# A four-layer graph network on one core: batch norm ahead and folded into weights, a fused ELU, and log-softmax by chunk and tile

## What is computed

```python
# second block, after two convolutions
return jax.nn.log_softmax(h, axis=1)
# third block
h = (x @ W).reshape(N, H, C)                      # 4 heads of 32
...                                               # attention weights alpha from x @ W and att_src, att_dst
out = jax.ops.segment_sum(h[src] * alpha[:, :, None], dst, num_segments=N).reshape(N, H * C)
out = out + x @ W_res + bias
out = (out - bn_mean) * jax.lax.rsqrt(bn_var + BN_EPS) * bn_gamma + bn_beta
return jax.nn.elu(out)
```

## Time and profile before

| | us |
|---|---|
| median of 3 runs | 2975.74 |
| the runs | 2973.39 to 2977.03 |
| the profiled execution | 2972.53 |
| its span | 2970.7 |
| TensorE busy in it | 2514.9 (85%) |
| VectorE busy | 2453.1 (83%) |
| ScalarE busy | 1969.7 (66%) |

### The profile page before, as it was taken

One profiled execution on the slowest core, in us unless ns is written; L12 is line 12 of the kernel. 1 busy time (PEld: TensorE's weight loads), 2 busy tenths in 40 slices (PEclk: granted clock), 3 DMA queues, 4 the chain that ended last, 5 costly groups with the idle time before them and its releaser, 6 DMA issues. The chain is left out here.

```text
span 2970.7 us, 60024 instructions
## 1 busy us (share of the span) xinstructions
PE 2514.9 (85%) x19214; PEld 2069.2 (70%) x19214; DVE 2453.1 (83%) x5349; ACT 1969.7 (66%) x3974; POOL 222.5 (7%) x487
## 2 busy tenths in 40 slices
PE   0888888775489888789884799999999999989998
PEld 0555555554467666667663599979998799979997
DVE  7998999953579999899997788868887788878886
ACT  1666666640368888788884577766777677767775
POOL 3000000000000000000000111101110111101110
PEclk9998999987788999899997899999999999999999
DMA  1232332355123333633330343414333243324332
GB/s 44 77 119 108 114 126 101 134 240 131 74 101 109 109 109 109 182 118 111 109 109 5 124 148 129 150 69 150 136 133 129 96 148 129 130 91 144 137 134 83
DMA packets 86664, 349.26 MB, mean 118 GB/s; under 512 B 47241, under 2 KB 59329, under 8 KB 59584
## 3 DMA queue, kind: packets, MB, share of 16 engines
q1 hardware_dynamic: 86437, 346.34, 33.2%
HBM read 279.61 MB, written 65.67 MB: 116 GB/s over the span
## 5 line engine op out<-in xcount | busy, mean ns | idle before, releaser
L1902 ACT ACTIVATE awcol<-aturned 125x500 fp32r<-125x500 f32 (+2 forms) x652 | 373.9, 573 | 310.7 <-PE aturned L1809 307.4
L1999 DVE TENSOR_TENSOR awcol<-aturned,awcol 125x500 fp32r<-125x500 f32 (+2 forms) x652 | 427.7, 656 | 114.7 <-ACT awcol L1902 109.3
L1821 PE MATMUL asum<-awcol,vals_high 125*128 125x512 f32 (+1 forms) x1300 | 477.6, 388 | 0.0
L1389 PE MATMUL gturned<-ident,grow 125*125 125x125 f32 x2500 | 409.7, 305 | 3.8 <-ACT grow L1299 3.8
L1821 PE MATMUL asum<-awcol,vals_low 125*128 125x256 f32 x1300 | 402.8, 319 | 0.0
L1389 PEld LDWEIGHTS gturned<-ident,grow 125*125 125x125 f32 x2500 | 332.5, 204 | 81.7 <-issue 77.1
L1226 DVE CUSTOM_DVE_ANT_0 grow<-grow,bias 125x3125 f32<-125x3125 f32 x100 | 341.7, 3417 | 25.1 <-DMA bias<-bias_dram 10.9
L1217 DVE SCALAR_TENSOR_TENSOR grow<-line,a_dst 125x3125 f32<-125x3125 f32 x100 | 347.6, 3476 | 13.2 <-PE gturned L1389 13.2
L1299 ACT ACTIVATE grow<-grow,neg 125x3125 f32<-125x3125 f32 x100 | 290.5, 2905 | 90.6 <-DVE neg L1229 90.5
L1339 PE MATMUL gparts<-gwcol,h_mem 125*32 125x125 f32 x5000 | 244.0, 290 | 106.1 <-ACT gwcol L1312 106.1
L1312 ACT ACTIVATE gwcol<-gturned 125x1000 f32<-125x1000 f32 x300 | 281.8, 1002 | 17.6 <-PE gturned L1389 17.5
(11 more groups left out here) (312 smaller groups left out, 5016.9 us busy)
## 6 DMA issues: line engine op xcount, KB each, us to landing
abias<-bias_dram SPq DMA_DIRECT2D x100, 1562.5 KB, 6.5
bias<-bias_dram SPq DMA_DIRECT2D x50, 1562.5 KB, 6.5
bias_dram<-lnrow SPq DMA_DIRECT2D x25, 1562.5 KB, 5.2
counts_dram<-pair SPq DMA_DIRECT2D x13, 1562.5 KB, 6.5
pair<-counts_dram SPq DMA_DIRECT2D x13, 1562.5 KB, 16.3
line<-lines_dram SPq DMA_DIRECT2D x4, 1367.2 KB
fixed<-kp SPq DMA_DIRECT2D x250, 4.0 KB, 1.7
agg<-counts_dram SPq DMA_DIRECT2D x2, 1367.2 KB
```

Source lines behind the costliest of these rows:

```text
L1389: last = pe.transpose(bank[q % RING][:, j // 4, j % 4 * T:(j % 4 + 1) * T], row[n % RING][:, t * T:(t + 1) * T], ident[0:T, 0:T])
L1821: last = pe.matmul(sum_ps[e][:, 0:n_cols], left[:, t, :], buffer[:, j * wide:j * wide + n_cols], start=(t == 0 and n == 0), stop=(t == NT ...
L1902: act.activation(operand(P, e, u, 0), turned(P, e, u), ACT.Copy).then_inc(high_copied, 1)
L1999: dve.tensor_tensor(operand(P, e, u, 1), turned(P, e, u), operand(P, e, u, 0).bitcast(FP32), ALU.subtract).then_inc(low_made, 1)
```

## The change

In block `soft`, VectorE takes a chunk out and makes its row maximum at once, with the sign turned. ScalarE takes the exponential tile by tile, with the maximum as its bias, and sums it in the same instruction. The logarithm is taken once; maximum and logarithm are joined in one small subtraction, and 25 instructions add y and this shift to x, tile by tile.

The five rows of batch norm are loaded in the head of the third block, ahead of the bias tables, to all 128 partitions. VectorE and ScalarE make the factor there, VectorE multiplies it into `wres` and into a copy of W (`w_scaled`) from which the values are made, and leaves the constant in one partition (`shift`). In the tail TensorE adds the constant to the residual product: a second product of one row of ones and `shift` into the same bank. The root and the loads leave the tail. The ELU is two additions: x + max(v, 0), and x + (exp(min(v, 0)) - 1).

```diff
         act_columns(act, banks, "v", vcols, rows=HID)
-        act.wait_ge(soft_in, 1)
-        act.activation(work[:, :, :], work[:, :, :], ACT.Exp).then_inc(soft_out, 1)
-        act.wait_ge(soft_in, 2)
-        act.activation(small[:, 1, :], small[:, 1, :], ACT.Ln).then_inc(soft_out, 1)
+        for c in range(NC):
+            act.wait_ge(soft_in, c + 1)
+            for t in tiles_of(c):
+                last = act.activation(work[:, t, :], agg[0:T, t * D:(t + 1) * D], ACT.Exp, bias=small[:, 0, t:t + 1],
+                                      accum_out=small[:, 1, t:t + 1])
+        last.then_inc(soft_out, 1)
+        act.wait_ge(soft_out, 1)
+        act.activation(logs[:, :], small[:, 1, :], ACT.Ln).then_inc(soft_out, 1)
         norms[1].scalar(act)

     @block.vector
     def _(dve):
         m = Marks(dve_done)
         y = agg[0:T, 0:NT * D].rearrange("p (t d) -> p t d", d=D)
+        top, shift = small[:, 0, :], small[:, 2, :]
         for c in range(NC):
             ts = tiles_of(c)
+            part = slice(ts[0], ts[-1] + 1)
             bank = banks.full(dve, "y", c)
-            dve.tensor_tensor(y[:, ts[0]:ts[-1] + 1, :], rows_view(bank, c, D),
-                              cb2[:, :].unsqueeze(1).broadcast_to([T, len(ts), D]), ALU.add).then_inc(banks.read["dve"], 1)
-        banks.done(dve, "y")
-
-        big, total = small[:, 0, :], small[:, 1, :]
-        chain(dve, m, dve.tensor_reduce(big, y, AX.X, ALU.max))
-        chain(dve, m, dve.tensor_tensor(y, y, each(big, everything, D), ALU.subtract))
-        dve.tensor_copy(work[:, :, :], y).then_inc(soft_in, 1)
-        dve.wait_ge(soft_out, 1)
-        dve.tensor_reduce(total, work[:, :, :], AX.X, ALU.add).then_inc(soft_in, 1)
-        chain(dve, m, dve.tensor_tensor(x[:, :, :], x[:, :, :], y, ALU.add))
+            chain(dve, m, dve.tensor_tensor(y[:, part, :], rows_view(bank, c, D),
+                                            cb2[:, :].unsqueeze(1).broadcast_to([T, len(ts), D]), ALU.add))
+            dve.sem_inc(banks.read["dve"], 1)
+            dve.tensor_reduce(top[:, part], y[:, part, :], AX.X, ALU.max, negate=True).then_inc(soft_in, 1)
+        dve.wait_ge(soft_in, NC)
         dve.wait_ge(soft_out, 2)
-        chain(dve, m, dve.tensor_tensor(x[:, :, :], x[:, :, :], each(total, everything, D), ALU.subtract))
+        chain(dve, m, dve.tensor_tensor(shift, top, logs[:, :], ALU.subtract))
+        for t in range(NT):
+            last = dve.scalar_tensor_tensor(out=x[:, t, :], in0=y[:, t, :], scalar=shift[:, t:t + 1], in1=x[:, t, :],
+                                            op0=ALU.add, op1=ALU.add)
+        chain(dve, m, last)
         norms[1].vector(dve, m)
...
+shift = sbo("l2_shift", [1, D])
+ones = sbo("l2_ones", [1, T])
...
+w_scaled = sb("w2_scaled", [D, D])
+root_out = sem("l2_root_out")
...
         sp.dma_start(wres[:, :], G["L2_gnn_W_res"]).then_inc(weights_in, 16)
+        for j, name in enumerate(("bias", "bn_gamma", "bn_beta", "bn_mean", "bn_var")):
+            sp.dma_start(rows[:, j, :], G[f"L2_gnn_{name}"].unsqueeze(0).broadcast_to([128, D])).then_inc(rows_in, 16)
         load_bias(0)
...
                 m.inc(dve.tensor_scalar(att[:, k * HEADS:(k + 1) * HEADS], in_head[:, :], att_in[:, k:k + 1], None, ALU.mult))
+            bias_of, gamma, beta, mean, root = (rows[:, j, :] for j in range(5))
+            chain(dve, m, dve.memset(ones[:, :], 1.0))
+            dve.wait_ge(rows_in, 80)
+            m.inc(dve.tensor_tensor(bias_of, bias_of, mean, ALU.subtract))
+            m.inc(dve.tensor_scalar(root, root, EPS, None, ALU.add))
+            dve.wait_ge(root_out, 1)
+            chain(dve, m, dve.reciprocal(root, root))
+            chain(dve, m, dve.tensor_tensor(gamma, gamma, root, ALU.mult))
+            chain(dve, m, dve.tensor_tensor(wres[:, :], wres[:, :], gamma, ALU.mult))
+            chain(dve, m, dve.tensor_tensor(w_scaled[:, :], w[:, :], gamma, ALU.mult))
+            chain(dve, m, dve.tensor_tensor(bias_of, bias_of, gamma, ALU.mult))
+            chain(dve, m, dve.tensor_tensor(shift[:, :], rows[0:1, 2, :], rows[0:1, 0, :], ALU.add))
             own_ps = ahead.full(dve, "own", 0)
...
         act.activation(w_att[:, :], here[:, 0:2 * HEADS], ACT.Copy).then_inc(ahead.read["act"], 1)
+        act.wait_ge(pre_dve, 6)
+        act.activation(rows[:, 4, :], rows[:, 4, :], ACT.Sqrt).then_inc(root_out, 1)
+        act.preload_act_table(ACT.Exp)
         broadcast_line(0)
...
+        pe.wait_ge(pre_dve, 10)
+        pe_rows(pe, ahead, "vals", [cols], [w_scaled[:, :]])
...
-                last = pe.matmul(res_ps[c][:, j * D:(j + 1) * D], cols[:, t * T:(t + 1) * T], wres[:, :], start=True, stop=True)
+                here = res_ps[c][:, j * D:(j + 1) * D]
+                pe.matmul(here, cols[:, t * T:(t + 1) * T], wres[:, :], start=True, stop=False)
+                last = pe.matmul(here, ones[:, :], shift[:, :], start=False, stop=True)
...
-    @block.sync
-    def _(sp):
-        for k, name in enumerate(("bias", "bn_gamma", "bn_beta", "bn_mean", "bn_var")):
-            sp.dma_start(rows[:, k, :], G[f"L2_gnn_{name}"].unsqueeze(0).broadcast_to([T, D])).then_inc(rows_in, 16)
...
         act.wait_ge(own_in, 1)
         act.activation(own[:, :, :], own[:, :, :], ACT.Exp).then_inc(own_out, 1)
-        act.wait_ge(root_in, 1)
-        act.activation(rows[:, 4, :], rows[:, 4, :], ACT.Sqrt).then_inc(root_out, 1)
         act.wait_ge(elu_in, 1)
-        act.activation(work[:, :, :], work[:, :, :], ACT.Exp).then_inc(elu_out, 1)
+        act.activation(low[:, :, :], low[:, :, :], ACT.Exp).then_inc(elu_out, 1)
...
-        dve.wait_ge(rows_in, 80)
-        dve.tensor_scalar(rows[:, 4, :], rows[:, 4, :], EPS, None, ALU.add).then_inc(root_in, 1)
...
-        bias, gamma, beta, mean, root = (rows[:, k, :] for k in range(5))
-        dve.wait_ge(root_out, 1)
-        chain(dve, m, dve.tensor_tensor(bias, bias, mean, ALU.subtract))
-        chain(dve, m, dve.reciprocal(root, root))
-        chain(dve, m, dve.tensor_tensor(gamma, gamma, root, ALU.mult))
-        chain(dve, m, dve.tensor_tensor(bias, bias, gamma, ALU.mult))
-        chain(dve, m, dve.tensor_tensor(beta, beta, bias, ALU.add))
-        chain(dve, m, dve.tensor_tensor(work[:, :, :], work[:, :, :], every(1), ALU.mult))
-        chain(dve, m, dve.tensor_tensor(work[:, :, :], work[:, :, :], every(2), ALU.add))
-
-        chain(dve, m, dve.tensor_scalar(res[:, :, :], work[:, :, :], 0.0, -1.0, ALU.max, ALU.add))
-        dve.tensor_scalar(work[:, :, :], work[:, :, :], 0.0, None, ALU.min).then_inc(elu_in, 1)
-        chain(dve, m, dve.tensor_tensor(x[:, :, :], x[:, :, :], res[:, :, :], ALU.add))
+        dve.tensor_scalar(low[:, :, :], work[:, :, :], 0.0, None, ALU.min).then_inc(elu_in, 1)
+        chain(dve, m, dve.scalar_tensor_tensor(out=x[:, :, :], in0=work[:, :, :], scalar=0.0, in1=x[:, :, :], op0=ALU.max, op1=ALU.add))
         dve.wait_ge(elu_out, 1)
-        chain(dve, m, dve.tensor_tensor(x[:, :, :], x[:, :, :], work[:, :, :], ALU.add))
+        chain(dve, m, dve.scalar_tensor_tensor(out=x[:, :, :], in0=low[:, :, :], scalar=-1.0, in1=x[:, :, :], op0=ALU.add, op1=ALU.add))
         norm.vector(dve, m)
```

More of the change, by code:

```diff
@@ L730, in layers_0_1 @@
         parts = sb("parts0", [T, NT, 6])
-        small = sb("small0", [T, 2, NT])
+        small = sb("small0", [T, 3, NT])
         w1, w2, b1, b2, cw1, cb1, cw2, cb2 = (G[k] for k in ("w1_0", "w2_0", "b1_0", "b2_0", "cw1", "cb1", "cw2", "cb2"))
@@ L1056, in layers_0_1 @@
             work = soft.enter_context(nc.sbuf_tensor("work0", [T, NT, D], FP32))
+            logs = soft.enter_context(nc.sbuf_tensor("soft_logs", [T, NT], FP32))
             banks = bank_set(nc, soft, "l1", [("v", NC, "act"), ("y", NC, "dve")])
@@ L1145, in graph_attention @@
                            ("vals", NC, "act"), ("lines", 1, "act"), ("line1", NC, "act")])
-            weights_in = sem("l2_weights_in")
+            weights_in, rows_in = sem("l2_weights_in"), sem("l2_rows_in")
+            rows = sb("rows2", [128, 5, D])
             lines_made, lines_out = sem("lines_made"), sem("lines_out")
@@ L1371, in _ @@
                     broadcast_line(0)
-                    pe_rows(pe, ahead, "vals", [cols], [w[:, :]])
+                    pe.wait_ge(pre_dve, 10)
+                    pe_rows(pe, ahead, "vals", [cols], [w_scaled[:, :]])
                     pe.wait_ge(lines_made, 1)
@@ L1402, in graph_attention @@
             work = sb("work2", [T, NT, D])
+            low = sb("low2", [T, NT, D])
             stat = sb("stat2", [T, 4, NT])
             total = sb("total", [T, NT, HEADS])
-            rows = sb("rows2", [T, 5, D])
-            rows_in = sem("l2_rows_in")
-            root_in, root_out = sem("l2_root_in"), sem("l2_root_out")
             elu_in, elu_out = sem("elu_in"), sem("elu_out")
@@ L1411, in graph_attention @@
             own_in, own_out = sem("own_in"), sem("own_out")
-            res = sb("res", [T, NT, D])
```

(3 more changed lines are left out.)

## The result

| | before | changed |
|---|---|---|
| median of 20 runs, us | 2977.03 | 2968.42 |
| the runs | 2971.80 to 2981.94 | 2962.33 to 2979.19 |
| ratio | | 0.9974 (0.9966 to 0.9982) |
| span of the profiled execution | 2970.7 | 2973.3 |

By the ratio the change makes the kernel 0.26% faster, 7.7 us (the medians differ by 8.6). I had forecast 25.9 us and a median of 2949.8; the time lies outside the range of 2945 to 2956, the sign is right. The changed kernel's profiled execution is one of the slower ones of its kernel, so I compare stretches, not spans. They are: from VectorE's first bias addition in `soft` to the next statistics (soft); from VectorE's first instruction in the third block's head to its first in the units (head); the units; from VectorE's first instruction in the tail to the next statistics (tail).

What follows compares the result with a forecast made beforehand. TensorE's chain held 41% of the span, in the untouched transformer; VectorE bounded `soft` and tail. Savings of 8.7 (`soft`) + 0 (head) + 6.0 + 11.2 (tail) = 25.9 us gave a median of 2949.8, range 2945 to 2956.

Steps and rivals of the forecast that it cites:

- my signs of being wrong: VectorE waiting for the residual product; a gap after the logarithm's table load; own terms later after the line; untouched stretches moving over 2 us.
- I had weighed another: The skill's rule on ScalarE table loads: a drain of about 1.38 us beside a 1.28 load at every switch, in `soft`.
- Softmax: In `soft`, the layer norm starts at 790.6 in place of 799.34: 8.7 us less, between 2.0 and 10.7.
- Rival (a): Small instructions dearer in `soft`: exponentials at 0.58 cost 4.8 us more, 2954.6; additions at 0.34 as well, 2956.6; chance 0.13.
- rival (c): In `soft`, ScalarE drains at the switch to the logarithm; a gap of 1.3 us would give 2951.1; chance 0.04.
- Head: Third block's head: loading and work on the batch norm's rows hide in VectorE's and ScalarE's waits, costing nothing.
- rival (b): TensorE's clock in the head comes out otherwise: 4.3 us earlier, 2945.5, or as much lost; chance 0.06, even both ways.
- My price for late rows: In the head, each us that the batch norm's rows land after 824.4 costs up to one us.
- Tail, VectorE's side: In the tail, no wait for the rows, 6.0 us less; batch norm's passes and the ELU's first pass go, 11.2 less.
- the ELU's second operations: In the tail, second operations added to the ELU's remaining passes; two passes could lose 0.1 us, left to the range.
- (d): The transformer runs slower because TensorE's clock comes back later after a shorter pause: 2984.8, slower by 0.3%; chance 0.02.
- (e): In the head the rows land past 846, behind the tables; the head loses 21.7 us, time 2971.5; chance 0.02.

## Why the prediction was wrong

**The step that failed** is this one of the tail: "The residual product doubles its records: 100 at 5.70 / 50 = 0.114 end at 1605.8. VectorE wants the first bank at 1614.37 - 6.0 = 1608.4 and the last after 1611; the product costs nothing unless a record of the one-row product takes over twice as long." I priced a product of one row by the row of a product of 128 rows, and named the bound at which it would matter without giving it a chance. The records took 34.1 us. In two parts: at the full clock a product beside one of another mode starts 0.41 after it, not 0.22, which makes 20.5 us of the whole; then the clock fell, and 0.72 made it 34. By the first alone the last bank would have come at 1616.7, some 3 us after VectorE wants it (1596.15 + 14.0 to its first addition + 3.3 for six more); worked out, not run. Both together cost 16.8 us of the 17.2.

The bound was even in the numbers: the last bank is wanted 17.3 us after the start, so with 128-row records at 0.114 any price over 0.23 for a one-row record was enough, or 0.17 as the mean of all hundred. The wait of VectorE for the residual product stood first among my signs of being wrong, and in no rival.

The Trainium skill has a rule that fits ("TensorEngine Tiling (Array Packing)", section "Key Properties"): changing the tiling mode drains TensorE. The same page's section "When to Use Tiling" gives row tiling to contractions of 64 and of 32. The runs agree with both together: 0.41 us from product to product with 1, 32 and 64 rows beside 128, and 0.22 with 96 and 128. That a product of few rows changes the mode by itself is my inference from this; no profile names the mode. Nor does a run part a drain from a weight load that can't start ahead. It was the rule that spoke against this change, and I had weighed another.

Why the clock stayed low is shown in part: few rows at work are enough to keep it down (`soft`), and the gaps' own share is open.

**Softmax: right.** 8.25 us less, where I had 8.7. The exponentials took 9.7 (9.8), the additions by tile 6.65 (6.6). Most of the missing 0.4 lies between the logarithm's end at 788.75 and the first addition by tile at 789.43, where I had counted some 0.25. Rival (a) fell, and so did rival (c), the drain at the table's switch: a load at 787.22, the logarithm at 788.52.

**Head: right in what it said of the rows, short by 1.2 us.** The last of the five loads landed 5.3 us after its issue, VectorE's part was over at 820.9, 3.5 us before the own terms, and the units began no later. They even began 1.2 us sooner, a gain that I had put at nothing and left to rival (b): the head takes 24.8 us in both profiles of the kernel before, at a mean granted clock of 0.65, and 23.5 in the changed kernel, at 0.68. Ten of the thirteen profiles with the new softmax have 23.5, three have 24.8 to 25.2; with the old softmax and the new third block it is 24.9. So the gain comes with the shorter softmax, and not always. My price for late rows, up to one us for each after 824.4, was too high: 2.9 us more were covered.

**Tail, VectorE's side: right.** Without the product's fault the tail is 26.7 us, as 43.9 less 17.2 makes it (the 26.4 that I gave counts from ScalarE's exponential, 0.3 later); the wait for the rows, the batch norm's passes and the first of the ELU's went as counted, and the ELU's second operations cost nothing (3.48 and 3.49).

**The sum.** 8.7 + 0 + 6.0 + 11.2 - 16.8 = 9.1 us, against 7.7 (5.4 to 10.1) measured; by the stretches it is 8.25 + 1.2 + 0.4 = 9.9. With the product mended 25.9 stand against 27 (22.6 to 31.3), and here two small misses, 0.4 too much in `soft` and 1.2 too little in the head, partly cancel. Rivals (d) and (e) did not come: the stretch behind the tail took 1332.5 to 1333.6 in all profiles.

## What to carry to other kernels

A small product added between large ones is not priced by their row: look first whether its contraction has 64 rows or fewer beside products of 128, and pad it to the full rows if it has; here 128 rows of 1/128 in place of one row of 1 are worth 16.8 us in the tail, at no cost that a profile shows. And where cover hides an added step, divide the cover by its count and ask what price for one would use it up; if no row bounds that price from above, it deserves a chance of its own.

## What the runs showed of the hardware that I had not expected

- An alternation of 128 with 1, 32 or 64 rows costs 0.19 us a product at the full clock (0.41 against 0.22) and 0.29 at the lower (0.72 against 0.43). With 96 rows it costs nothing.
- TensorE fell to its lower clock level, a granted clock of 0.50, while it was busy without a gap with products of 16 rows in `soft`, before the change as after it. In one profile it then stayed there for 8.5 us of such products; with products of 128 rows it came back after 3.4.
- A product of 32-bit floats with one row costs as much per moving column as one with 128: 0.11 a record of 128 columns at the full clock.
